# Second attention: the vector engine's squares one operation later, and the copy of the weighted sums moved from ScalarE to VectorE

## The chip, the cores and the metric

The kernel runs on one core of one Trainium2 chip. The metric is device time in microseconds (us) of one execution, the median of several. Lower is better. The engines are named as in the profile: PE (TensorE, matmuls; PEld is its weight loads), DVE (VectorE), ACT (ScalarE), POOL (GpSimd) and SP (SyncE, which only issues DMAs here).

## The reference, cut to what matters

The program is a stack of six layers over 4096 tokens of width 128: mixture of experts, causal attention, two mixtures of experts, a second attention, and a last mixture of experts. The change touches only the second attention. It is computed for each of 64 heads (4 batches of 16 heads, 1024 tokens each, 8 numbers to a head):

```python
S = jnp.einsum('bhnd,bhmd->bhnm', Q, K) / dh ** 0.5
W_tau = jax.nn.softmax(S, axis=-1)
W_sigma = 1.0 / ((1.0 + jnp.abs(S) / b_) ** 2 + t_ ** 2)
W_sigma = W_sigma / W_sigma.sum(axis=-1, keepdims=True)
tau = jnp.einsum('bhnm,bhmd->bhnd', W_tau, V)
sigma = jnp.einsum('bhnm,bhmd->bhnd', W_sigma, V)
f = 0.5 * tau + 0.5 * sigma
```

So every score is used twice: once through an exponential with the row's maximum taken off, and once as |S|, squared with an offset, then inverted.

## The kernel before, in words

`attend_both` (L1665 to L1979) holds five instruction streams written out by hand, one for each engine, which meet only through semaphores. Each engine works through its own stream in order: an instruction that waits holds up everything behind it on that engine.

The unit is a slot. A slot handles two blocks of 128 tokens (i = 0 and i = 1, its two halves) of a head, four slots to a head, 256 in all, plus a few at the end that only finish. One slot `j` works on different slots' data at once, each operation at its own lag (`LS, LT, LE, LP = 4, 6, 6, 7`):

- lag 0, the maxima: PE makes scores in PSUM tile `pm` (L1800); DVE reduces them to a row's maximum `mx` (L1958). Once in each half.
- lag 4, the absolute values: PE makes scores in `pa`; DVE clears their sign bit into the SBUF tile `sg` (L1967). Once in each half. Then, once in each slot, `sg` gets its square, sg times (sg + b): POOL does columns 0 to 831 of each half, in two instructions, first `shifted` = sg + b (L1758, "the shift" below) and then sg times `shifted` (L1761, "the product"); DVE does the columns 832 to 1023 of each half in one `scalar_tensor_tensor` (L1973, "the square" below).
- lag 6, the exponentials: PE makes scores in `pb`, ACT exponentiates them into `pt` (L1880), once in each half; ACT also turns the squares into weights with Ln (L1895, first half, which waits for both squares) and Exp (L1899, second half).
- lag 7 and 8, the weighing: PE multiplies V with `pt` and `sg` into one PSUM tile `po`, four matmuls in each half (L1817, `weigh`). In slot j's half i = 0 it does the second block of slot j-8, in half i = 1 the first block of slot j-7.

`pm`, `pa` and `pb` are single tiles. PE's order in each half is `pm`, `pb`, `pa`, `weigh`; a matmul group into `pm` waits for the reduction of the one before, one into `pa` for the absolute values before. DVE's order in a slot is maximum, absolute values, maximum, absolute values, square.

The slots of a head differ. Below they are called A (j mod 4 = 0), B, C and D (j mod 4 = 3):

- D: the weighing in its first half ends a head. ACT copies `po` to `osb` (L1887) after its first exponential. In the second half `weigh` starts the next head in the same `po`, so it waits for that copy (`o_sb`, L1815). After it PE turns `osb` with four transposes into `ptr` (L1863), which also waits for the copy.
- A: DVE normalises the turned sums between its first maximum and its first absolute values (`output`, L1934 to L1948, four small instructions, "the output"), and at the slot's end makes the negated maxima of another head (`negated`, L1914 to L1921, four small instructions, "the negation"). POOL makes two small copies for the next head (L1747, L1749) before its shift.

All these orders are written out by hand; no planner sets them.

Of the kernel before, what the change touches and what calls it, by code (L numbers as in the profile page):

```python
# [11 lines left out]
ALU = mybir.AluOpType  # L12
# [8 lines left out]
TT = T // P  # L21
# [1648 lines left out]
def attend_both(nc, tag, V, F, par, qd, kd, ident, stacks, cleared):  # L1670
# [11 lines left out]
    with ExitStack() as ctx:  # L1682
# [28 lines left out]
        def at(it, j, lag):  # L1711
            s = UNROLL * it + (j - lag)
            return None if isinstance(s, int) and not 0 <= s < SLOTS else s

        def head(it, j, lag):

            return RING * it + (j - lag) // PER
# [10 lines left out]
        def some(x, least=1):  # L1728

            return not (isinstance(x, int) and x < least)  # L1730

        with nc.Block() as block:

            @block.gpsimd
            def _(pool):
                nc.gpsimd.memset(Vh[:], 0.0).then_inc(vh_cleared, 1)
                pool.wait_ge(vh_cleared, 1)

                def body(it, j):
                    s = at(it, j, LS)  # L1740
                    if s is None:
                        return
                    h = head(it, j, LS)
                    if (j - LS) % PER == 0:
                        if some(h, 2):
                            pool.wait_ge(pv_done, TT * (h - 1))
                        nc.gpsimd.tensor_copy(parh[:, ((j - LS) // PER) % RING, :], par[:, h, :])\  # L1747
                            .then_inc(par_ready, 1)
                        nc.gpsimd.tensor_copy(Vh[:, ((j - LS) // PER) % 2, :, 0:DH + 1], V[:, h, :, :])\  # L1749
                            .then_inc(vh_ready, 1)  # L1750
                    buf = sg[(j - LS) % 4]
                    if some(s):
                        pool.wait_ge(sq_pool, s)
                    pool.wait_ge(par_ready, h + 1)
                    pool.wait_ge(abs_done, 2 * s + 2)
                    pool.nop(nofuse=True)
                    b2 = parh[:, ((j - LS) // PER) % RING, 0:1]
                    nc.gpsimd.tensor_scalar(shifted[:], buf[:, :, 0:CUT], b2, 1.0, ALU.add, ALU.mult)\  # L1758
                        .then_inc(shift_done, 1)
                    pool.wait_ge(shift_done, s + 1)  # L1760
                    nc.gpsimd.tensor_tensor(buf[:, :, 0:CUT], buf[:, :, 0:CUT], shifted[:], ALU.mult)\  # L1761
                        .then_inc(sq_pool, 1)

                slots(pool, body)
# [104 lines left out]
            @block.scalar  # L1869
            def _(act):  # L1870
                nc.scalar.preload_act_table_set("natural_log_exp_and_others")

                def body(it, j):
                    st, se, so = at(it, j, LT), at(it, j, LE), at(it, j, LP + 1)
                    for i in range(2):
                        if st is not None:
                            act.wait_ge(tau_mm, 2 * st + i + 1)
                            if some(st, 4):
                                act.wait_ge(pv_done, 2 * (st - 4) + i + 1)
                            nc.scalar.activation(pt[(j - LT) % 4][:, i, :], pb[:], ACT.Exp, scale=SC)\  # L1880
                                .then_inc(tau_exp, 1)
                        if i == 0 and so is not None and (j - LP - 1) % PER == PER - 1:
                            h = head(it, j, LP + 1)
                            act.wait_ge(pv_done, TT * h + TT)
                            if some(h):
                                act.wait_ge(o_turned, h)
                            nc.scalar.activation(osb[:], po[:], ACT.Copy).then_inc(o_sb, 1)  # L1887
                        if se is not None:
                            buf = sg[(j - LE) % 4]
                            if i == 0:  # L1890
                                h = head(it, j, LE)
                                act.wait_ge(sq_pool, se + 1)
                                act.wait_ge(sq_dve, se + 1)
                                act.wait_ge(par_ready, h + 1)
                                nc.scalar.activation(buf[:], buf[:], ACT.Ln,  # L1895
                                                     bias=parh[:, ((j - LE) // PER) % RING, 1:2]).then_inc(ln_done, 1)
                            else:
                                act.wait_ge(ln_done, se + 1)
                                nc.scalar.activation(buf[:], buf[:], ACT.Exp, scale=-1.0).then_inc(sig_done, 1)  # L1899

                slots(act, body)

            @block.vector
            def _(dve):
# [18 lines left out]
                def output(it, j, n):  # L1923

                    if (j - LP - 2) % PER != PER - 1 or at(it, j, LP + 2) is None:
                        return
                    h = head(it, j, LP + 2)
                    o = ptr[:].rearrange("p (c q k) -> p c q k", c=4, q=4)
                    scale = rz[:].unsqueeze(3).broadcast_to([P, 4, 4, DH])
                    if n == 0:  # L1930
                        dve.wait_ge(o_turned, h + 1)
                        if some(h):
                            dve.wait_ge(weighed, 2 * h)
                        nc.vector.reciprocal(rz[:], o[:, :, :, DH]).then_inc(rz_done, 1)  # L1934
                    if n == 1:
                        dve.wait_ge(rz_done, h + 1)
                        if some(h):
                            dve.wait_ge(f_done, h)
                        nc.vector.tensor_tensor(fw[:], o[:, :, 0:2, 0:DH], scale[:, :, 0:2], ALU.mult)\
                            .then_inc(weighed, 1)  # L1940
                        nc.vector.tensor_tensor(o[:, :, 2:4, 0:DH], o[:, :, 2:4, 0:DH], scale[:, :, 2:4], ALU.mult)\
                            .then_inc(weighed, 1)
                    if n == 2:
                        dve.wait_ge(weighed, 2 * h + 2)
                        nc.vector.tensor_tensor(F[:, :, h, :].rearrange("p (s c) d -> p s c d", s=2),
                                                o[:, :, 2:4, 0:DH].rearrange("p c s d -> p s c d"),
                                                fw[:].rearrange("p c s d -> p s c d"), ALU.add)\
                            .then_inc(f_done, 1)  # L1948

                def body(it, j):  # L1950
                    sm, ss = at(it, j, 0), at(it, j, LS)
                    for i in range(2):
                        if sm is not None:
                            t = 2 * (j % PER) + i
                            dve.wait_ge(max_mm, 2 * sm + i + 1)
                            if i == 0 and j % PER == 0 and some(sm, 2 * PER):
                                dve.wait_ge(rows_turned, head(it, j, 0) - 1)
                            nc.vector.tensor_reduce(mx[:, (j // PER) % 2, t:t + 1], pm[:], AX.X, ALU.max)\  # L1958
                                .then_inc(max_red, 1)
                        if i == 0:  # L1960
                            for n in range(3):
                                output(it, j, n)
                        if ss is not None:
                            dve.wait_ge(abs_mm, 2 * ss + i + 1)
                            if some(ss, 4):
                                dve.wait_ge(pv_done, 2 * (ss - 4) + i + 1)
                            nc.vector.tensor_scalar(sg[(j - LS) % 4][:, i, :].bitcast(I32), pa[:].bitcast(I32),  # L1967
                                                    SIGN_OFF, None, ALU.bitwise_and).then_inc(abs_done, 1)
                    if ss is not None:
                        h, buf = head(it, j, LS), sg[(j - LS) % 4]  # L1970
                        dve.wait_ge(abs_done, 2 * ss + 2)
                        dve.wait_ge(par_ready, h + 1)
                        nc.vector.scalar_tensor_tensor(buf[:, :, CUT:T], buf[:, :, CUT:T],  # L1973
                                                       parh[:, ((j - LS) // PER) % RING, 0:1], buf[:, :, CUT:T],
                                                       ALU.add, ALU.mult).then_inc(sq_dve, 1)
                    negated(it, j)

                slots(dve, body)
# [165 lines left out]
```

## Time and profile before

| | |
|---|---|
| median of 3 runs | 3061.43 us (3060.11 to 3062.47) |
| the profiled execution's own time | 3088.97 us |
| its span, first to last instruction | 3086.9 us |
| busy DVE, PE, ACT, POOL | 2546.7, 2456.0, 2250.8, 1999.4 us (83, 80, 73, 65% of the span) |
| the second attention, maxima first to last (L1958) | starts at 1241.3, last at 2770.2 us |

Busy is the time in which an engine executes; the rest is idle, mostly waiting. Shares over the whole span mix stages; the change must be read from the stretch of about 1240 to 2810 us, where the page shows DVE, ACT and POOL 9 tenths busy in each slice and PE 8 or 9. A timeline row gives start, duration, engine, line and operation, the tile written, the tile read, their shapes, and in brackets how long the engine was idle before it and who ended that.

### The profile page before, as it was taken

How to read it: one execution, taken by the hardware profiler on the slowest of the kernel's cores; microseconds unless marked ns; L12 is line 12 of the kernel's file. 1: busy time of each engine (PE TensorE's matmuls, PEld its weight loads, DVE VectorE, ACT ScalarE, POOL GpSimd, SP SyncE). 2: the span in 40 equal slices, each digit the busy share in tenths (PEclk: the TensorE clock that was granted, in tenths of full speed). 3: DMA queues.
4: the chain of work that ended last, by engine and by line, in shares of the span. 5: the costliest groups of instructions: out<-in, count | busy, mean ns of one | idle time of the engine just before them, and what ended most of it. 6: DMA issues, size and time to landing. Idle time of an engine off the chain costs nothing. (4 is left out here: it accounts for less than half of the span.)

```text
span 3086.9 us, 61248 instructions
## 1 busy us (share of the span) xinstructions
PE 2456.0 (80%) x18614; PEld 1025.5 (33%) x18614; DVE 2546.7 (83%) x4239; ACT 2250.8 (73%) x2441; POOL 1999.4 (65%) x1364
## 2 busy tenths in 40 slices
PE   2545999998476994688888888888888888885798
PEld 2542333334374662122222222222222222222466
DVE  4566888885467657799999999999999999996765
ACT  4332777776364553499999999999999999994454
POOL 4520222222453651599999999999999999995365
PEclk9976999999596997699999999999999999997799
DMA  3213101100111002000000000000000000000000
GB/s 110 58 51 102 30 27 29 28 28 10 41 55 28 1 0 83 19 13 14 14 12 12 12 14 13 12 12 12 15 12 12 12 13 14 12 4 0 1 11 17
DMA packets 77121, 74.42 MB, mean 24 GB/s; under 512 B 16096, under 2 KB 57576, under 8 KB 76880
## 3 DMA queue, kind: packets, MB, share of 16 engines
q1 hardware_dynamic: 72720, 64.20, 7.0%
q0 software_dynamic: 4288, 8.82, 0.9%
q8 instruction: 58, 0.95, 0.1%
q14 instruction: 55, 0.45, 0.1%
HBM read 47.77 MB, written 24.42 MB: 23 GB/s over the span
## 5 line engine op out<-in xcount | busy, mean ns | idle before, releaser
L1761 POOL TENSOR_TENSOR a_sg<-a_sg,a_shifted 128x1664 f32<-128x1664 f32 x256 | 955.4, 3732 | 21.4
L1958 DVE TENSOR_REDUCE a_mx<-a_pm 128x1 f32<-128x1024 f32 x512 | 619.5, 1210 | 22.0 <-PE a_pm L1800 21.9
L1967 DVE TENSOR_SCALAR a_sg<-a_pa 128x1024 int32<-128x1024 int32 x512 | 619.4, 1210 | 4.1 <-PE a_pa L1800 3.8
L1880 ACT ACTIVATE a_pt<-a_pb 128x1024 f32<-128x1024 f32 x512 | 523.5, 1023 | 108.6 <-PE a_pb L1800 108.4
L1817 PE MATMUL a_po<-a_pt,a_Vh 128*32 128x512 f32 x2048 | 540.6, 607 | 2.2 <-ACT a_sg L1899 2.2
L1817 PE MATMUL a_po<-a_sg,a_Vh 128*32 128x512 f32 x2048 | 540.6, 607 | 0.0
L1758 POOL TENSOR_SCALAR a_shifted<-a_sg,a_parh 128x1664 f32<-128x1664 f32 x256 | 470.4, 1837 | 102.3 <-DVE a_sg L1967 64.8
L1895 ACT ACTIVATE a_sg<-a_sg,a_parh 128x2048 f32<-128x2048 f32 x256 | 511.9, 1999 | 0.0
L1899 ACT ACTIVATE a_sg<-a_sg 128x2048 f32<-128x2048 f32 x256 | 489.9, 1914 | 0.0
L1800 PE MATMUL a_pm<-all_K,all_Q 96*128 96x512 bf16 x1024 | 315.9, 391 | 151.2 <-DVE a_mx L1958 124.1
L1579 ACT ACTIVATE a_pt<-a_ring 128x1024 f32<-128x1024 f32 (+2 forms) x384 | 313.6, 846 | 165.7 <-PE a_ring L1506 162.4
L1656 DVE TENSOR_REDUCE a_mx<-a_ring 128x2 f32<-128x1024 f32 (+3 forms) x384 | 359.3, 955 | 75.4 <-PE a_ring L1489 51.1
L1800 PE MATMUL a_pa<-all_Q,all_K 96*128 96x512 bf16 x1024 | 310.8, 385 | 83.5 <-DVE a_sg L1967 66.3
L1414 POOL TENSOR_SCALAR_AFFINE_SELECT a_pt<-a_pt 128x256 f32<-128x256 f32 x256 | 104.0, 406 | 370.7 <-ACT a_pt L1579 370.3
L1800 PE MATMUL a_pb<-all_Q,all_K 128*128 128x512 bf16 x1024 | 307.5, 381 | 6.0 <-ACT a_pt L1880 5.4
L1973 DVE SCALAR_TENSOR_TENSOR a_sg<-a_sg,a_parh 128x384 f32<-128x384 f32 x256 | 234.1, 915 | 15.7 <-POOL a_parh L1747 2.8
L1800 PEld LDWEIGHTS a_pm<-all_K,all_Q 96*128 96x128 bf16 x1024 | 63.5, 97 | 546.6 <-DVE a_mx L1958 523.3
L1523 PE MATMUL a_po<-a_pt,a_Vh 128*32 128x384 f32 (+3 forms) x1920 | 190.7, 435 | 1.9 <-POOL a_pt L1414 1.8
L900 ACT ACTIVATE f_sg<-f_psg 128x512 f32<-128x512 f32 x176 | 104.5, 594 | 116.7 <-PE f_psg L859 116.7
L1800 PEld LDWEIGHTS a_pa<-all_Q,all_K 96*128 96x128 bf16 x1024 | 79.3, 97 | 273.2 <-DVE a_sg L1967 232.7
L954 DVE TENSOR_TENSOR f_su<-f_psu,f_sg 128x512 f32<-128x512 f32 x144 | 98.7, 687 | 79.8 <-PE f_psu L859 74.5
L1506 PE MATMUL a_ring<-all_Q,all_K 51*128 51x512 bf16 (+2 forms) x768 | 131.8, 341 | 36.9 <-DVE a_mx L1656 32.1
(272 smaller groups left out, 4612.9 us busy)
## 6 DMA issues: line engine op xcount, KB each, us to landing
all_Q<-q_parts SPq DMA_DIRECT2D x256, 48.0 KB
all_K<-k_parts SPq DMA_DIRECT2D x256, 48.0 KB
k_parts<-p_parts SPq DMA_DIRECT2D x16, 384.0 KB, 2.6
all_Q<-a_rows SPq DMA_DIRECT2D x384, 2.0 KB
e_recs<-routed_rows SPq DMA_DIRECT2D x70, 64.5 KB, 1.8
n_xn<-expert_rows SPq DMA_DIRECT2D x16, 256.0 KB, 4.4
q_parts<-p_parts SPq DMA_DIRECT2D x16, 192.0 KB, 2.3
q_parts<-p_parts SPq DMA_DIRECT2D x8, 384.0 KB, 2.6
```

Source lines behind the costliest of these rows:

```text
L1579: nc.scalar.activation(pt[n % 4][:, :, ga:gb, c * P:CH], of_weight(y)[:, :, 0:(gb - ga) * width].rearrange("p u (g n) -> p u g n", n=width ...
L1656: nc.vector.tensor_reduce(mx[:, j % 2, half, :, strip_at(t)], of_maximum(y)[:, :, 0:min(CH, (t + 1) * P - half * CH)], AX.X, ALU.max).then ...
L1758: nc.gpsimd.tensor_scalar(shifted[:], buf[:, :, 0:CUT], b2, 1.0, ALU.add, ALU.mult)\
L1761: nc.gpsimd.tensor_tensor(buf[:, :, 0:CUT], buf[:, :, 0:CUT], shifted[:], ALU.mult)\
L1800: last = nc.tensor.matmul(out[:, lo:lo + CH], lhsT[0:rows_, t * P:(t + 1) * P], rhs[0:rows_, lo:lo + CH], start=True, stop=True)
L1817: last = nc.tensor.matmul(po[32 * q:32 * q + 32, :], Vh[:, ((j - lag) // PER) % 2, t, :], wts[:, i, half * CH:(half + 1) * CH], start=(t = ...
L1880: nc.scalar.activation(pt[(j - LT) % 4][:, i, :], pb[:], ACT.Exp, scale=SC)\
L1895: nc.scalar.activation(buf[:], buf[:], ACT.Ln, bias=parh[:, ((j - LE) // PER) % RING, 1:2]).then_inc(ln_done, 1)
L1899: nc.scalar.activation(buf[:], buf[:], ACT.Exp, scale=-1.0).then_inc(sig_done, 1)
L1958: nc.vector.tensor_reduce(mx[:, (j // PER) % 2, t:t + 1], pm[:], AX.X, ALU.max)\
L1967: nc.vector.tensor_scalar(sg[(j - LS) % 4][:, i, :].bitcast(I32), pa[:].bitcast(I32), SIGN_OFF, None, ALU.bitwise_and).then_inc(abs_done, 1)
L1973: nc.vector.scalar_tensor_tensor(buf[:, :, CUT:T], buf[:, :, CUT:T], parh[:, ((j - LS) // PER) % RING, 0:1], buf[:, :, CUT:T], ALU.add, AL ...
```

## The change

Three edits. The DVE square of a slot is issued one operation later: not at the end of the slot, but in the next slot behind its first maximum (and ahead of the output). POOL's product gets a second wait: besides its own shift it now waits for the DVE square of the same slot (`sq_dve`). The copy of `po` to `osb` leaves ACT; DVE does it in slot D between its second maximum and its second absolute values.

```diff
@@ pool
                     pool.wait_ge(shift_done, s + 1)
+                    pool.wait_ge(sq_dve, s + 1)
                     nc.gpsimd.tensor_tensor(buf[:, :, 0:CUT], buf[:, :, 0:CUT], shifted[:], ALU.mult)\
                         .then_inc(sq_pool, 1)
@@ act
-                        if i == 0 and so is not None and (j - LP - 1) % PER == PER - 1:
-                            h = head(it, j, LP + 1)
-                            act.wait_ge(pv_done, TT * h + TT)
-                            if some(h):
-                                act.wait_ge(o_turned, h)
-                            nc.scalar.activation(osb[:], po[:], ACT.Copy).then_inc(o_sb, 1)
@@ dve
+                def copy_out(it, j):
+
+                    if (j - LP - 1) % PER != PER - 1 or at(it, j, LP + 1) is None:
+                        return
+                    h = head(it, j, LP + 1)
+                    dve.wait_ge(pv_done, TT * h + TT)
+                    if some(h):
+                        dve.wait_ge(o_turned, h)
+                    nc.vector.tensor_copy(osb[:], po[:]).then_inc(o_sb, 1)
+
+                def square(it, j):
+
+                    s = at(it, j, LS + 1)
+                    if s is None:
+                        return
+                    h, buf = head(it, j, LS + 1), sg[(j - LS - 1) % 4]
+                    dve.wait_ge(abs_done, 2 * s + 2)
+                    dve.wait_ge(par_ready, h + 1)
+                    nc.vector.scalar_tensor_tensor(buf[:, :, CUT:T], buf[:, :, CUT:T],
+                                                   parh[:, ((j - LS - 1) // PER) % RING, 0:1], buf[:, :, CUT:T],
+                                                   ALU.add, ALU.mult).then_inc(sq_dve, 1)
@@ dve, body
                         if i == 0:
+                            square(it, j)
                             for n in range(3):
                                 output(it, j, n)
+                        else:
+                            copy_out(it, j)
@@ dve, after the two halves
-                    if ss is not None:
-                        h, buf = head(it, j, LS), sg[(j - LS) % 4]
-                        dve.wait_ge(abs_done, 2 * ss + 2)
-                        dve.wait_ge(par_ready, h + 1)
-                        nc.vector.scalar_tensor_tensor(buf[:, :, CUT:T], buf[:, :, CUT:T],
-                                                       parh[:, ((j - LS) // PER) % RING, 0:1], buf[:, :, CUT:T],
-                                                       ALU.add, ALU.mult).then_inc(sq_dve, 1)
                     negated(it, j)
```

## Rows read from the trace of the kernel before

**Rows 1.** Busy us of each engine in the steady stretch (window view).
```profile
core 0: us, PE busy (x) PEld busy (x) DVE busy (x) ACT busy (x) POOL busy (x), PEclk, DMA share, GB/s
1340.00:2700.00 1360.00, 1175.15 (x6624) 312.56 (x6625) 1332.29 (x1582) 1294.56 (x964) 1278.71 (x565) 1.00 0.04 13
```

**Rows 2.** Groups by line: busy us, mean ns of one, idle before and its releasers.
```profile
L1758 POOL TENSOR_SCALAR a_shifted<-a_sg,a_parh 128x1664 f32<-128x1664 f32 x256 | 470.4, 1837 | 102.3 <-DVE a_sg L1967 64.8 <-POOL a_sg L1761 32.2
...
L1973 DVE SCALAR_TENSOR_TENSOR a_sg<-a_sg,a_parh 128x384 f32<-128x384 f32 x256 | 234.1, 915 | 15.7 <-POOL a_parh L1747 2.8
...
L1887 ACT ACTIVATE a_osb<-a_po 128x512 f32<-128x512 f32 x64 | 38.2, 597 | 6.0 <-PE a_po L1817 3.6
```

**Rows 3.** Timeline of DVE from slot D's second maximum to the next D's.
```profile
2001.27 1.21 DVE L1958 TENSOR_REDUCE a_mx<-a_pm 128x1 f32<-128x1024 f32 x1
2002.40 1.21 DVE L1967 TENSOR_SCALAR a_sg<-a_pa 128x1024 int32<-128x1024 int32 x1
2003.65 1.20 DVE L1973 SCALAR_TENSOR_TENSOR a_sg<-a_sg,a_parh 128x384 f32<-128x384 f32 x1
2004.77 1.21 DVE L1958 TENSOR_REDUCE a_mx<-a_pm 128x1 f32<-128x1024 f32 x1
2005.90 0.24 DVE L1934 RECIPROCAL a_rz<-a_ptr 128x16 f32<-128x16 f32 x1
...
2006.93 1.22 DVE L1967 TENSOR_SCALAR a_sg<-a_pa 128x1024 int32<-128x1024 int32 x1
...
2009.20 1.21 DVE L1967 TENSOR_SCALAR a_sg<-a_pa 128x1024 int32<-128x1024 int32 x1
2010.45 0.62 DVE L1973 SCALAR_TENSOR_TENSOR a_sg<-a_sg,a_parh 128x384 f32<-128x384 f32 x1
...
2012.14 1.20 DVE L1958 TENSOR_REDUCE a_mx<-a_pm 128x1 f32<-128x1024 f32 x1
...
2016.77 0.62 DVE L1973 SCALAR_TENSOR_TENSOR a_sg<-a_sg,a_parh 128x384 f32<-128x384 f32 x1
2017.30 1.22 DVE L1958 TENSOR_REDUCE a_mx<-a_pm 128x1 f32<-128x1024 f32 x1
...
2025.33 1.21 DVE L1958 TENSOR_REDUCE a_mx<-a_pm 128x1 f32<-128x1024 f32 x1
```

**Rows 4.** Timeline of POOL beside them.
```profile
2000.69 3.74 POOL L1761 TENSOR_TENSOR a_sg<-a_sg,a_shifted 128x1664 f32<-128x1664 f32 x1
2004.68 1.68 POOL L1758 TENSOR_SCALAR a_shifted<-a_sg,a_parh 128x1664 f32<-128x1664 f32 x1 [0.25 <-POOL a_sg L1761]
2006.45 3.73 POOL L1761 TENSOR_TENSOR a_sg<-a_sg,a_shifted 128x1664 f32<-128x1664 f32 x1
...
2010.62 1.97 POOL L1758 TENSOR_SCALAR a_shifted<-a_sg,a_parh 128x1664 f32<-128x1664 f32 x1
...
2016.90 2.00 POOL L1758 TENSOR_SCALAR a_shifted<-a_sg,a_parh 128x1664 f32<-128x1664 f32 x1 [0.51 <-DVE a_sg L1967]
```

**Rows 5.** Timeline of PE, second half of slot D and on into A.
```profile
2001.41 0.60 PE L1800 MATMUL a_pa<-all_Q,all_K 96*128 96x512 bf16 x2
2001.94 0.62 PE L1817 MATMUL a_po<-a_pt,a_Vh 128*32 128x512 f32 x2
...
2002.94 0.66 PE L1863 MATMUL a_ptr<-all_ident,a_osb 128*128 128x128 f32 x4
2003.43 0.60 PE L1800 MATMUL a_pm<-all_K,all_Q 96*128 96x512 bf16 x2
...
2006.04 0.60 PE L1800 MATMUL a_pm<-all_K,all_Q 96*128 96x512 bf16 x2
```

**Rows 6.** Timeline of both engines where a maximum waited for its scores.
```profile
1296.13 0.60 PE L1800 MATMUL a_pm<-all_K,all_Q 96*128 96x512 bf16 x2
...
1296.77 1.22 DVE L1958 TENSOR_REDUCE a_mx<-a_pm 128x1 f32<-128x1024 f32 x1 [0.31 <-PE a_pm L1800]
```

**Rows 7.** Groups by line of DVE: instructions that read PSUM and write SBUF.
```profile
L963 DVE TENSOR_TENSOR f_hid<-f_psm,f_su 128x512 f32<-128x512 f32 x144 | 97.7, 680 | 1.7 <-POOL all_V L820 1.7
...
L1124 DVE COPY all_V<-p_psv 128x128 f32<-128x128 f32 x32 | 7.0, 281 | 0.0
```

More of the change, by code:

```diff
@@ L1873, in body @@
                 def body(it, j):
-                    st, se, so = at(it, j, LT), at(it, j, LE), at(it, j, LP + 1)
+                    st, se = at(it, j, LT), at(it, j, LE)
                     for i in range(2):
```

## The prediction, made before the changed kernel ran

> **What bounds the kernel now.** I first read the window view of the steady stretch: of 1360 us DVE is busy 1332, ACT 1295, POOL 1279, PE 1175 [rows 1]. DVE is 98% full, so whatever is added to it, or makes it wait, should show. Next, the groups by line: the square has a mean of 915 ns [rows 2], but the timeline shows only two durations, 0.62 us (A, B) and 1.20 us (C, D) [rows 3]. POOL's timeline says why: the 1.20 us square starts at 2003.65, while a product runs until 2000.69 + 3.74 = 2004.43, and it ends 0.42 us after that; the 0.62 us ones start before POOL's shift, and that shift then takes 1.97 or 2.00 us instead of 1.68 [rows 4]. So square and POOL exclude each other in both orders: whoever is second stands until the first is done. DVE loses 0.58 us in two slots of four.
>
> The head's period is 2025.33 - 2001.27 = 24.06 us [rows 3]. POOL is close behind: product start to next product 2006.45 - 2000.69 = 5.76 us where it never waits, and 0.19 us once a head for its two copies (product end 2010.18 to shift 2010.62, 0.44 instead of 0.25) [rows 4]: 4 x 5.76 + 0.19 = 23.23 us. The slack of POOL is 0.8 us a head.
>
> **The pieces, from the rows.** Issue to issue, DVE's maximum and absolute values take 1.13 us each (2001.27 to 2002.40), though each lasts 1.21; a free square 0.53 (2016.77 to 2017.30), a held one until 0.09 before its end; the output 2006.93 - 2005.90 = 1.03; the negation 2012.14 - 2010.45 - 0.53 = 1.16 [rows 3]. POOL: end of product to shift 0.25, end of shift to product 0.09, absolute values done to shift 2016.90 - 2016.77 + 0.03 = 0.16 [rows 3, 4]. PE: `pa` to `weigh` 0.53, `weigh` 1.00, transposes 0.49 (2002.94 to 2003.43); `pm` starts 0.06 after a maximum ends (2005.98 to 2006.04) [rows 3, 5], and a maximum that waits starts 0.64 after `pm` (1296.13 to 1296.77) [rows 6].
>
> **The change, part by part.** I write the new schedule of one head with the second maximum of slot D at 0.
>
> *The copy, slot D.* Off ACT: 0.60 us once a head [rows 2]. ACT idles 65 of 1360 us already [rows 1] and ends no wait of DVE or POOL, so this earns nothing. On DVE the nearest row of this size that reads PSUM and writes SBUF is 680 ns for 128x512; a 128x128 copy is 281 ns, and the two differ by 1.04 ns a column, a rate that a copy should share [rows 7]. Bounds: ACT's 0.60 and 0.75. I take 0.68, 0.60 issue to issue. It runs from 1.13 to 1.81. Its own wait is free: the last weighing lies ahead of `pm` in PE's order. But behind it hangs `weigh` of the second half, which must not overwrite `po`. Before, it started 2001.94 - 2001.27 = 0.67 after the maximum [rows 3, 5]; now at 1.81 + 0.06 = 1.87. Then transposes at 2.87, next `pm` at 3.36, and DVE's maximum of slot A at 4.00. DVE, which no longer has a square there, is free at 1.13 + 0.60 + 1.13 = 2.86: it stands for 1.14 us. The cover that hid PE's chain before was the square (the maximum came 3.50 after the last one).
>
> *Slot D's square and slot A.* Absolute values done at 1.73 + 1.21 = 2.94; shift 3.10 to 4.78; square issued at 4.00 + 1.13 = 5.13, POOL idle then, ends 5.75. The new wait holds the product until 5.85 (0.10 after the square; bounds 0.06 and 0.25), ends 9.58. DVE: output from 5.66, absolute values 6.69, maximum 7.82, absolute values 8.95, negation 10.08, maximum of B 11.24, square 12.37 to 12.99. The shift of A starts at the later of 9.58 + 0.44 and 10.16 + 0.21, 10.37, and ends 12.05, so this square too is free; product 13.09 to 16.82.
>
> *Slots B and C.* B's absolute values start at 12.90 and 15.16. The maximum of C comes not 1.13 behind: PE needs the first absolute values done (1.21), 0.05, `pa` 0.53, `weigh` 1.00, `pm` 0.64, in all 3.43 after 12.90, so 16.33, and its square is issued at 17.46. But POOL began B's shift at 16.82 + 0.25 = 17.07, until 18.75. The square stands behind it and ends at 18.75 + 0.42 = 19.17, 1.71 us long. Only then can the product start, 19.27 to 23.00. Before, nothing stood between shift and product. C repeats it 6.18 later: shift 23.25 to 24.93, square held until 25.35, product to 29.18. DVE goes on at 25.26, and the second maximum of D comes at 26.39. (POOL's next shift is then due at 29.43, DVE's work at 29.49: the schedule closes.)
>
> *Sum.* 26.39 - 24.06 = 2.33 us a head. The maxima of 64 heads fill 1529 us, 63.5 periods; the first and last slots lack weighing or maxima, so I count 62: 62 x 2.33 = 144 us. The profiled execution is 3088.97 us, with 2.07 around its span of 3086.9; it would become 3233. It lies 27.5 above the median of 3061.43. The added time is in engines' instructions and waits, so it is put on the median: 3205 us.
>
> **The Trainium skill.** That a square stands behind a *shift* is my extension: in the rows the square waits for a product (two SBUF inputs), and the shift (one tensor) waits for a square [rows 4]. The Trainium skill, "SBUF — State Buffer", section "Who interferes with whom", says that a DVE instruction with two SBUF inputs contends with a GpSimd one that reads SBUF, and that the second to issue blocks fully. By that rule the shift holds the square, which is the 3205 above; if a one-input instruction held nothing, the sum would be the 3072 of rival 1. The trace agrees in the order it has.
>
> **Bounds.** A shift that does not hold a square gives the lower end (rival 1). The wait's release, twice on the chain (A's and B's product), 0.06 or 0.25 instead of 0.10: -0.1 to +0.3 a head. The copy 0.60 or 0.75: -0.08 to +0.07. PE's restart after a wait 0.06, or up to 0.4: up to +0.3. So 2.15 to 3.0 a head, 3195 to 3247.
>
> **Rivals.**
> 1. *Squares are not behind shifts.* Either a shift doesn't hold them, or POOL is a little later than worked out (the margin in B and C is 17.46 - 17.07 = 0.39 us) and the square goes first. Unheld: after 17.46 follow 17.99, 21.42, 22.55, 23.08, and the period is 24.21: +0.15, 62 x 0.15 = 9 us, 3071 to 3072. Square first, and then, as now, held 0.58 behind a product in two slots: +1.31, 81 us, 3143. For it: the small margin. Against it: both engines hang on the same square's end, so the margin doesn't drift. Chance 0.13.
> 2. *Faster: the copy is hidden and the squares are free.* If PE lost nothing by `weigh` waiting, DVE would need 24.21 - 1.14 = 23.07, POOL 23.23 binds, -0.83 a head: -51 us, 3010. It decides if DVE's idle before A's maximum is near zero. Against it: PE goes from `weigh` through transposes to `pm` without a gap today [rows 5]. Chance 0.05.
> 3. *POOL becomes the sole bound and is woken late.* If its product starts 0.5 after a square instead of 0.10, the two waits on the chain add 0.8 a head: 3.13 x 62 = 194, 3255. Against it: 0.16 for the shift today. Chance 0.12.
>
> Forecast 0.70, its own range 3190 to 3230. The range 3120 to 3245 takes in the upper part of rival 1 and the lower part of rival 3. A measurement can tell about 0.2%, 6 us: faster 0.05 (rival 2), same 0.03 (the low edge of rival 1), slower 0.92.
>
> **What would show it.** In the after trace: the square 0.62 us in two slots of a head (for D and A) and about 1.7 us in the two others, mean near 1.16; the shift 1.68 everywhere; POOL idle before its product, released by the square, 1.0 us twice and 0.5 us twice a head; DVE idle 1.1 us before A's maximum on `pm`, and PE's weights for `po` waiting for DVE's `osb` 1.2 us; the copy at 0.68 us; period 26.4 us. It is wrong if squares behind a shift last 0.62 us, if slot A's maximum isn't late, or if the period is under 25.

## The result and the profile after

The changed kernel takes 3261.56 us (median of 4 runs, 3260.98 to 3266.71) against 3061.36 for the kernel before: ratio 1.066, 95% interval 1.0647 to 1.0672. It is 200.2 us slower; 143.6 were forecast (3205, range to 3245). The direction held, and so did the steps of the hand schedule wherever the granted clock was 1.00; one term was missing, about 56 us, and the range ended 17 us short of the result.

All of it lies in the second attention. Its maxima now run from 1212.2 to 2942.3 us, 1730.1 us; before, 1241.3 to 2770.2, 1528.9. That is 201.2 us more. (In the profiled execution of the kernel before, the stages ahead of it took 29 us more than in that of after, and its own time lay 27.5 us above its median; so putting the difference on the median was right.)

The window view of after, columns as in [rows 1]:

```profile
core 0: us, PE busy (x) PEld busy (x) DVE busy (x) ACT busy (x) POOL busy (x), PEclk, DMA share, GB/s
1340.00:2640.00 1300.00, 1043.46 (x5481) 281.51 (x5573) 1190.03 (x1380) 1074.50 (x763) 1039.90 (x478) 0.94 0.04 11
```

No engine is full any more: DVE fell from 98 to 92%, POOL from 94 to 80%. Everything became less busy while the time grew, so the engines wait for each other more than before. And the granted clock is 0.94 where it was 1.00, which was not forecast.

The groups by line (columns as in [rows 2]) name the waits:

```profile
L1762 POOL TENSOR_TENSOR a_sg<-a_sg,a_shifted 128x1664 f32<-128x1664 f32 x256 | 954.6, 3729 | 269.4 <-DVE a_sg L1963 268.9
...
L1818 PE MATMUL a_po<-a_pt,a_Vh 128*32 128x512 f32 x2048 | 573.6, 640 | 77.5 <-DVE a_osb L1953 75.2 <-ACT a_sg L1894 2.2
...
L1758 POOL TENSOR_SCALAR a_shifted<-a_sg,a_parh 128x1664 f32<-128x1664 f32 x256 | 424.3, 1657 | 102.1 <-DVE a_sg L1987 69.4 <-POOL a_sg L1762 32.6
L1975 DVE TENSOR_REDUCE a_mx<-a_pm 128x1 f32<-128x1024 f32 x512 | 621.3, 1214 | 145.8 <-PE a_pm L1801 145.8
...
L1963 DVE SCALAR_TENSOR_TENSOR a_sg<-a_sg,a_parh 128x384 f32<-128x384 f32 x256 | 297.1, 1161 | 0.5 <-POOL a_parh L1747 0.3
...
L1953 DVE COPY a_osb<-a_po 128x512 f32<-128x512 f32 x64 | 43.1, 674 | 12.7 <-PE a_po L1818 12.7
```

The shift is no longer held (mean 1657 ns, it was 1837 [rows 2]); the square's mean is 1161 ns (1.16 forecast, 915 before); POOL stands 269 us for it; PE stands 75 us for the copy; the copy is 674 ns (0.68 forecast). DVE stands 146 us for `pm` ahead of its maxima.

Here is DVE of after from slot B's square to slot A, the rows that answer to [rows 3]:

```profile
2005.11 1.69 DVE L1963 SCALAR_TENSOR_TENSOR a_sg<-a_sg,a_parh 128x384 f32<-128x384 f32 x1
...
2011.31 1.68 DVE L1963 SCALAR_TENSOR_TENSOR a_sg<-a_sg,a_parh 128x384 f32<-128x384 f32 x1
...
2014.05 1.21 DVE L1975 TENSOR_REDUCE a_mx<-a_pm 128x1 f32<-128x1024 f32 x1
2015.18 0.67 DVE L1953 COPY a_osb<-a_po 128x512 f32<-128x512 f32 x1
2015.78 1.21 DVE L1987 TENSOR_SCALAR a_sg<-a_pa 128x1024 int32<-128x1024 int32 x1
2018.12 1.23 DVE L1975 TENSOR_REDUCE a_mx<-a_pm 128x1 f32<-128x1024 f32 x1 [1.14 <-PE a_pm L1801]
2019.26 0.61 DVE L1963 SCALAR_TENSOR_TENSOR a_sg<-a_sg,a_parh 128x384 f32<-128x384 f32 x1
...
2040.42 1.21 DVE L1975 TENSOR_REDUCE a_mx<-a_pm 128x1 f32<-128x1024 f32 x1
...
2046.24 1.22 DVE L1975 TENSOR_REDUCE a_mx<-a_pm 128x1 f32<-128x1024 f32 x1 [2.89 <-PE a_pm L1801]
```

And POOL beside it, to be read with [rows 4]:

```profile
2004.75 1.65 POOL L1758 TENSOR_SCALAR a_shifted<-a_sg,a_parh 128x1664 f32<-128x1664 f32 x1 [0.26 <-POOL a_sg L1762]
2006.95 3.72 POOL L1762 TENSOR_TENSOR a_sg<-a_sg,a_shifted 128x1664 f32<-128x1664 f32 x1 [0.55 <-DVE a_sg L1963]
2010.93 1.66 POOL L1758 TENSOR_SCALAR a_shifted<-a_sg,a_parh 128x1664 f32<-128x1664 f32 x1 [0.25 <-POOL a_sg L1762]
2013.14 3.72 POOL L1762 TENSOR_TENSOR a_sg<-a_sg,a_shifted 128x1664 f32<-128x1664 f32 x1 [0.56 <-DVE a_sg L1963]
...
2020.02 3.73 POOL L1762 TENSOR_TENSOR a_sg<-a_sg,a_shifted 128x1664 f32<-128x1664 f32 x1 [1.21 <-DVE a_sg L1963]
...
2027.13 3.73 POOL L1762 TENSOR_TENSOR a_sg<-a_sg,a_shifted 128x1664 f32<-128x1664 f32 x1 [1.11 <-DVE a_sg L1963]
```

The square at 2005.11 is issued 0.36 us into the shift of 2004.75 to 2006.40, and ends 0.40 after it. The product of 2006.95 could have started at 2006.49 (0.09 after the shift). DVE's copy of 2015.18 runs inside the product of 2013.14 to 2016.86 and still takes 0.67 us: the product does not hold it. From D's second maximum (2014.05) to A's first (2018.12) are 4.07 us (4.00 forecast); to D's second maximum of the next head (2040.42) are 26.37 us (26.39 forecast).

The next slot D is another matter: its A comes at 2046.24, 5.82 us after 2040.42, and DVE stands 2.89 us. PE of after in that slot:

```profile
2042.37 1.07 PE L1818 MATMUL a_po<-a_pt,a_Vh 128*32 128x512 f32 x2 [1.21 <-DVE a_osb L1953]
...
2043.20 1.10 PE L1818 MATMUL a_po<-a_pt,a_Vh 128*32 128x512 f32 x2
...
2044.24 1.12 PE L1864 MATMUL a_ptr<-all_ident,a_osb 128*128 128x128 f32 x4
2045.15 1.06 PE L1801 MATMUL a_pm<-all_K,all_Q 96*128 96x512 bf16 x2
```

The window view gives the granted clock of the two slots, the late one first:

```profile
2042.00:2048.00 6.00, 5.63 (x22) 1.99 (x26) 3.11 (x5) 1.51 (x2) 2.88 (x2) 0.50 0.00 0
2015.50:2020.00 4.50, 4.00 (x27) 1.43 (x28) 3.36 (x5) 2.17 (x3) 3.01 (x2) 1.00 0.00 0
```

In the late slot TensorE is at 1.2 GHz, in the other at 2.4. The chain on which DVE stands is weighing, transposes and `pm`. From the first weighing to `pm` it takes 2.78 us (2042.37 to 2045.15) instead of 1.49 (1.00 + 0.49 [rows 5]), and from `pm` to DVE's maximum 1.09 (2045.15 to 2046.24) instead of 0.64: 1.74 us more in all. 31 of the 63 head periods are like this. The trace has 31 stretches at 0.5 while these heads run, 200.6 us together; each begins 1.0 to 1.9 us after the second maximum of a slot D, one in each late head and none in the others.

The clock falls at 2041.6. In the 5.2 us ahead of that PE did much the same as at the same place of the head before, where the clock stayed up (columns as in [rows 1]):

```profile
2010.00:2015.20 5.20, 3.52 (x18) 0.84 (x17) 5.20 (x6) 4.63 (x5) 4.39 (x3) 1.00 0.00 0
2036.40:2041.60 5.20, 3.49 (x18) 0.82 (x17) 5.20 (x6) 4.63 (x5) 4.39 (x3) 1.00 0.00 0
```

### The profile page after: what moved, and what is told of

It is laid out like the page before. It is cut to its first block and busy times, and to the rows that moved or that the text cites. A ratio compares the mean times of both kernels' runs of the same rounds, so it can differ in the third digit from the quotient of the medians.

```text
span 3259.3 us, 61437 instructions
## 1 busy us (share of the span) xinstructions
PE 2519.3 (77%) x18487; PEld 1047.2 (32%) x18614; DVE 2643.7 (81%) x4303; ACT 2227.9 (68%) x2377; POOL 1952.2 (60%) x1364
## 5 line engine op out<-in xcount | busy, mean ns | idle before, releaser
L1818 PE MATMUL a_po<-a_pt,a_Vh 128*32 128x512 f32 x2048 | 573.6, 640 | 77.5 <-DVE a_osb L1953 75.2
L1818 PE MATMUL a_po<-a_sg,a_Vh 128*32 128x512 f32 x2048 | 573.5, 640 | 0.0
L1801 PE MATMUL a_pa<-all_Q,all_K 96*128 96x512 bf16 x1024 | 323.5, 399 | 232.2 <-DVE a_sg L1987 231.9
L1758 POOL TENSOR_SCALAR a_shifted<-a_sg,a_parh 128x1664 f32<-128x1664 f32 x256 | 424.3, 1657 | 102.1 <-DVE a_sg L1987 69.4
L1801 PE MATMUL a_pm<-all_K,all_Q 96*128 96x512 bf16 x1024 | 329.5, 405 | 53.6 <-DVE a_mx L1975 38.2
L1801 PE MATMUL a_pb<-all_Q,all_K 128*128 128x512 bf16 x897 | 291.9, 396 | 14.9 <-ACT a_pt L1881 7.6
L1963 DVE SCALAR_TENSOR_TENSOR a_sg<-a_sg,a_parh 128x384 f32<-128x384 f32 x256 | 297.1, 1161 | 0.5 <-POOL a_parh L1747 0.3
L1818 PEld LDWEIGHTS a_po<-a_pt,a_Vh 128*32 128x32 f32 x2048 | 78.5, 111 | 303.7 <-issue 240.2
```

Source lines behind the costliest of these rows:

```text
L1801: last = nc.tensor.matmul(out[:, lo:lo + CH], lhsT[0:rows_, t * P:(t + 1) * P], rhs[0:rows_, lo:lo + CH], start=True, stop=True)
L1818: last = nc.tensor.matmul(po[32 * q:32 * q + 32, :], Vh[:, ((j - lag) // PER) % 2, t, :], wts[:, i, half * CH:(half + 1) * CH], start=(t = ...
```

## Experiments

Each comparison is with the kernel before on the same chip. "The head's period" is read from D's second maximum to the next D's. What an experiment does not name is as in the kernel that it starts from. Except in e3, e7 and e8, every fourth head is 0.1 to 0.2 us longer than the period given.

**e1, the copy alone.** The kernel before, with `copy_out` of the change on DVE and ACT's copy gone; square and product as before.

> The kernel before with one edit: DVE copies the weighted sums out in slot D. The changed kernel's trace shows the head's period alternating between 26.4 or 26.6 us, as forecast, and 28.1 us, where the granted clock is at 0.5 from the copy's wait on. Theory (clock): TensorE's clock falls because PE does less in a head's period than before, held in slot D behind the copy and in B and C behind the held squares. Here only the copy's hold is left: A's maximum starts 4.00 us after D's second one instead of 3.50, so 24.03 + 0.5 = 24.55 us a head, 62 x 0.5 = 31 us, 3092 us, and the clock stays at 1.0 if slot D's hold alone is not enough to bring it down. Rival (the hold in slot D alone brings the clock down, whatever the other slots do): every second head gets 1.75 us more, 31 x 1.75 = 54, 3147 us. Rival (the copy costs nothing): 3061 us.

Measured: 3131.8 us, ratio 1.023 (1.0213 to 1.0247), +71.8. Where the clock stays up the head's period is 24.64 us (24.03 before); A's maximum comes 4.08 after D's (4.00 forecast). D's square, which now comes later, is no longer held (0.62 instead of 1.20 us), so the copy's 0.60 us on DVE costs next to nothing by itself, and the 0.6 us a head are DVE's wait for PE's chain. But 23 of 63 heads have 5.45 to 5.82 us from D's maximum to A's, 35.6 us more in all. So with the copy's hold alone the clock falls too, though not in every second head: between theory and rival. DVE's waits in two neighbouring heads of e1:

```profile
2015.44 1.22 DVE L1962 TENSOR_REDUCE a_mx<-a_pm 128x1 f32<-128x1024 f32 x1 [0.59 <-PE a_pm L1800]
...
2041.67 1.23 DVE L1962 TENSOR_REDUCE a_mx<-a_pm 128x1 f32<-128x1024 f32 x1 [2.08 <-PE a_pm L1800]
```

The first stands 0.59 us at full clock, the second 2.08 with the clock at 0.5 for a part of PE's chain.

**e2, the squares alone.** The change without its copy: `copy_out` out, ACT's copy back.

> The kernel before with the other two edits: DVE's square one operation later and POOL's product waits for it; the copy stays on ACT. The same hand schedule without the copy: D's square is issued at 3.93 after D's second maximum while the shift runs (3.04 to 4.69), is held to 5.11 instead of ending at 5.75, and all that follows is 0.64 us earlier: period 26.39 - 0.64 = 25.75 us, 62 x 1.72 = 107 us, 3168 us at full clock. Theory (clock): PE has no hold of 1.2 us in slot D, so the clock stays at 1.0 and 3168 us stands. Rival (the low activity of the whole period brings the clock down): 1.75 us more in each second head, 3222 us. Rival (the gain was lost to the copy alone, squares are harmless): 3061 us.

Measured: 3166.6 us, ratio 1.035 (1.0334 to 1.0368), +106.6, against 107 forecast. That this is so close is partly luck: the head's period is 25.70 us, not 25.75, and the theory on the clock was wrong. Its mean over the stretch is 0.98, not 1.00: there are 15 short stretches at 0.5, 51 us together. But each begins 7.6 to 8.6 us after D's second maximum, in slot A, behind the chain that DVE waits for; A's maximum comes at 2.79 to 2.90 in every head of the steady stretch. Nine heads are longer, by at most 0.6 us, about 4 us in all. So a low clock costs much only where PE's chain ends last; and it can fall without any hold by the copy. The groups of e2:

```profile
L1762 POOL TENSOR_TENSOR a_sg<-a_sg,a_shifted 128x1664 f32<-128x1664 f32 x256 | 955.4, 3732 | 178.0 <-DVE a_sg L1959 177.6
...
L1959 DVE SCALAR_TENSOR_TENSOR a_sg<-a_sg,a_parh 128x384 f32<-128x384 f32 x256 | 330.0, 1289 | 0.7 <-POOL a_parh L1747 0.6
```

The mean square is even longer than in the changed kernel (1289 against 1161): slot D's square, without the copy ahead of it, is issued in a shift too (1.20 us). POOL's waits for the square, 178 us, are 0.55 us in three slots of a head and 1.11 in the fourth.

**e3, the product without its new wait.** e2 with one line less:

```diff
                     pool.wait_ge(shift_done, s + 1)
-                    pool.wait_ge(sq_dve, s + 1)
```

> As e2_square_only, but POOL's product does not wait for DVE's square (they touch different columns). Theory (whoever waits takes the port at the next change of instruction, as the square did behind a product): the square goes first when the shift ends, the product stands 0.4 us behind it and shows as about 4.1 us; 0.1 us less idle in B, C and D: about 3150 us. Rival (the product, 0.09 us behind the shift, keeps the port): a square issued in a shift is held through the product too, 5.5 us long in B and C, the head's period grows by over 6 us: above 3450 us.

Measured: 3531.0 us, ratio 1.154 (1.1518 to 1.1557). The time is the rival's, the mechanism is neither's. DVE of e3, then POOL:

```profile
2003.06 0.74 DVE L1958 SCALAR_TENSOR_TENSOR a_sg<-a_sg,a_parh 128x384 f32<-128x384 f32 x1
...
2016.72 3.84 DVE L1958 SCALAR_TENSOR_TENSOR a_sg<-a_sg,a_parh 128x384 f32<-128x384 f32 x1
```

```profile
2001.75 1.65 POOL L1758 TENSOR_SCALAR a_shifted<-a_sg,a_parh 128x1664 f32<-128x1664 f32 x1 [3.99 <-DVE a_sg L1980]
2003.48 3.91 POOL L1761 TENSOR_TENSOR a_sg<-a_sg,a_shifted 128x1664 f32<-128x1664 f32 x1
...
2016.44 3.70 POOL L1761 TENSOR_TENSOR a_sg<-a_sg,a_shifted 128x1664 f32<-128x1664 f32 x1
```

The square of 2003.06 was issued in the shift, ended 0.40 after the shift's end at 2003.40, and the product issued at 2003.48 took 3.91 instead of 3.72: at a change of POOL's instruction the waiting square goes first, as my theory had it. But with POOL not waiting, about half of the squares (125 of 256 last over 3 us) come when the product has already begun, and are held through it: 3.84 us for the one of 2016.72. So the new wait is not a careless addition: once the square is issued late, it keeps the product from starting ahead of it, at the cost of POOL's waits given under e2. The granted clock of e3 was 0.89 over 1340 to 2640 us; how much of its time is the clock's is not separated here.

**e4, the changed kernel with PE kept busy.** In slot D, second half, ahead of the scores into `pa`. `fill` (a new helper, not shown) issues the same two matmuls, twice:

```diff
+                            if i == 1 and (j - LP - 1) % PER == PER - 1 and at(it, j, LP + 1) is not None:
+                                fill(pa, K[rs], Q[rs], 2 * ((j - LS) % PER) + i, 96)
                             scores(pa, K[rs], Q[rs], 2 * ((j - LS) % PER) + i, 96, abs_mm)
```

> The changed kernel with PE kept busy in slot D's second half: the two score matmuls into pa are issued three times with the same result, only the last signals DVE, four more matmuls of about 0.22 us at a point where PE then waits 1.2 us for the copy. Theory (clock): the matmuls take the place of waiting, the granted clock stays higher, and the missing 56 us come back: all heads at 26.4 to 26.6, 3207 us; if they only delay the fall, some heads stay at 28.1. Rival (the alternation of the heads' periods comes from a buffer or a DMA that turns every second head, and the clock falls as its result): 3262 us or, with PE's extra work on the path, above.

Measured: 3221.7 us, ratio 1.053 (1.051 to 1.0545): about 40 us faster than the changed kernel, by more work. 8 heads are still late, 12.6 us in all; without them it would be 3209 (3207 forecast). The window view of e4:

```profile
1340.00:2640.00 1300.00, 1058.68 (x5920) 293.37 (x5917) 1221.39 (x1417) 1103.14 (x783) 1067.14 (x491) 0.99 0.04 11
```

**e5, the same filler in e1.**

> e1_copy_only with the filler of e4_after_filled (in slot D's second half the two score matmuls into pa are issued three times with the same result). e1 has 24.64 us a head where the granted clock stays at 1.0, and about 1.5 us more in 24 of 63 heads whose slot D meets a clock of 0.5. Theory (clock): PE's wait for the copy brings the clock down; with the filler in its place nearly all heads take 24.64: 62 x 0.61 = 38 us over before, about 3099 us. Rival (the filler is on PE's path, or the clock falls for another reason): 3132 us or more.

Measured: 3097.2 us, ratio 1.012 (1.0104 to 1.0138), 34.6 us faster than e1. All heads of the steady stretch are at 24.64 to 24.77, and the clock, low as in every kernel when the second attention begins (until 1247 us), does not fall again in it. (The expectation speaks of 24 late heads of e1; they are 23, the 24th stretch at 0.5 lies in another slot.) The copy's cost without the clock is 36 us, with it 72. PE's mean busy share, from the window view of 1340 to 2640 us, does not order these runs: it is 85% in e1, where 23 heads are late, and 81% in e4, where 8 are.

```profile
1340.00:2640.00 1300.00, 1139.85 (x6382) 313.40 (x6374) 1247.41 (x1528) 1180.13 (x844) 1194.26 (x527) 1.00 0.04 12
```

**e6, the square ahead of the shift.** e2 with the wait moved:

```diff
                     pool.wait_ge(abs_done, 2 * s + 2)
+                    pool.wait_ge(sq_dve, s + 1)
                     pool.nop(nofuse=True)
...
                     pool.wait_ge(shift_done, s + 1)
-                    pool.wait_ge(sq_dve, s + 1)
```

> e2_square_only with the wait for DVE's square moved from POOL's product to POOL's shift. Theory (the loss of e2 is that a square issued in a shift is held to its end and POOL waits for it, 0.55 us of POOL's time in B and C and more in A and D): now the square goes ahead of the shift; it can only be held behind the product of the slot before, which it meets later in its run. Hand schedule: B and C take 5.57 + 0.42 = 6.0 us instead of 6.18, A and D are no longer held behind a shift, period about 25.2 us, 62 x 1.2 = 75 us, 3136 us. Rival (what costs is that POOL waits for DVE at all, wherever): POOL's shift and product then both stand behind a late square, the same or more than e2, 3167 us or above.

Measured: 3146.9 us, ratio 1.028 (1.0264 to 1.0298), 20 us better than e2, period 25.30 us (25.2 forecast). The square (mean 1215 ns) is now held behind the product of the slot before, B's and C's and D's; A's is free:

```profile
2005.69 1.55 DVE L1959 SCALAR_TENSOR_TENSOR a_sg<-a_sg,a_parh 128x384 f32<-128x384 f32 x1
...
2003.08 3.74 POOL L1762 TENSOR_TENSOR a_sg<-a_sg,a_shifted 128x1664 f32<-128x1664 f32 x1
```

The product ends at 2006.82, the square at 2007.24, 0.42 after it. With the wait in either of the two places, a square one operation late meets a POOL instruction in three slots of four; the order decides which.

**e7 and e8, less on POOL.** The kernel before with `CUT = 25 * T // 32` and `CUT = 24 * T // 32` instead of 26.

> The kernel before with CUT = 25 * T // 32: POOL squares 800 columns of each half instead of 832, DVE 224 instead of 192. Theory (in C and D the square stands 0.58 us behind a product that is late by POOL's own length): shift and product get 4% shorter, each square 0.07 us longer. Holds fall from 0.58 to about 0.38 in C and 0.31 in D: -0.2 -0.27 + 4 x 0.07 = -0.2 us a head, 12 us, 3048 us. Rival (DVE is the bound, so each column moved to it costs): +0.27 us a head, 3077 us.

> As e7_cut25 with CUT = 24 * T // 32. Theory: holds of about 0.15 in C and 0.04 in D: -0.43 -0.54 + 4 x 0.135 = -0.43 us a head, 27 us, 3034 us. Rival (DVE is the bound): +0.54 us a head, 3094 us.

Measured: e7 3053.9 us, ratio 0.9973 (0.9963 to 0.9984); e8 3045.1 us, ratio 0.9948 (0.9931 to 0.9965). Both are under 1% faster than the kernel before, by more than their intervals. The sign is the theory's; the sizes are 7 of 12 us and 16 of 27 us. The groups of e8:

```profile
L1761 POOL TENSOR_TENSOR a_sg<-a_sg,a_shifted 128x1536 f32<-128x1536 f32 x256 | 885.9, 3460 | 21.4
...
L1973 DVE SCALAR_TENSOR_TENSOR a_sg<-a_sg,a_parh 128x512 f32<-128x512 f32 x256 | 221.1, 863 | 14.3 <-POOL a_parh L1747 1.3
```

A third more columns, and the mean square is shorter than before (863 against 915 ns [rows 2]): holds went down faster than work went up. In C and D it still lasts 0.95 and 0.97 us where a free one lasts 0.75, so 0.2 is left of each hold where I had 0.15 and 0.04. (e7: C's and D's squares 1.07, a free one 0.69, so 0.38 is left of each where I had 0.38 and 0.31.)

## Why the prediction was right and wrong, point by point

- *Square and POOL exclude each other, the shift too.* Right. B's and C's squares last 1.69 and 1.68 us (1.71 forecast), D's and A's 0.60 to 0.61 (0.62). "A square behind a shift" had no row before. The Trainium skill, "SBUF — State Buffer", section "Who interferes with whom", says that a DVE instruction with two SBUF inputs contends with a GpSimd one that reads SBUF. The trace of after agrees: the square ends 0.40 us after the shift does. Rival 1 (squares not behind shifts) is out.
- *The product waits.* Right: 0.55 us idle in B and C, 1.21 and 1.11 in D and A (1.0 forecast).
- *The copy.* Right: 0.67 us, PE's weighing held for 1.21, A's maximum late by 1.14 at full clock, as worked out (0.68, 1.2 and 1.14).
- *The sum 2.33 us a head.* Right at full clock: 26.37 us, against 24.03 before (the 24.06 of the forecast was one of the longer heads), so 2.34. Every fourth head has 26.60; those 14 add 3 us.
- *Two edits, separately.* The squares alone cost 106.6 us (e2), the copy alone without the clock 35.8 (e5): 142.4 us, and 144 was the sum for both. (e2 holds about 4 us of low clock.)
- *Wrong: "PE's restart after a wait 0.06, or up to 0.4: up to +0.3", and no line on the clock at all.* The step that failed is the term of PE's chain in slot D: I took `weigh` 1.00, transposes 0.49 and 0.64 for `pm` from rows at a granted clock of 1.00 [rows 1, 5, 6] and did not ask whether PE, busy 1175 of 1360 us before and made to stand by both edits, keeps it. It did not. At 0.5 the three take 2.78 and 1.09, in all 3.87 us instead of 2.13, where the bound allowed 0.3. Over the 31 late heads the excess over 4.08 us is 53.5 us; 144 + 53.5 + 3 = 200.5, measured 200.2, closer than terms rounded to 0.01 us a head deserve. That it is the clock and not a buffer that turns every second head is shown by the stretches at 0.5, one in each late head and in no other, and by e4 and e5: adding matmuls where PE stood removed most or all of the late heads, and the low clock with them.
- *Rival 3 (POOL woken late)* gave 3255, near the result, by a cause that did not occur: POOL's product follows the square by 0.15 us. Rival 2 (faster) is out: PE's chain had no slack.

What stays open: why the clock falls in every second head in the changed kernel and in 23 of 63 in e1. PE's work of the few us before is the same in a head where it falls and in one where it does not (3.49 and 3.52 of 5.20 us busy). The runs show only that in these two kernels it falls around the copy's hold and stays up, or falls less often, when matmuls fill it; in e2, without that hold, it falls at another place.

## What to carry to other kernels

Where two engines exclude each other, look at which instruction of the other is running at the moment of issue; moving the short one later by one operation put it from a collision that costs 0.58 us into one that costs 1.07 and made the other engine wait too. A copy that frees an accumulator belongs on the engine that can do it at once: on DVE, which was 98% busy, it held the next matmuls by 1.2 us a head, and DVE's next maximum behind them. When a change makes TensorE stand, price its chain at the lower clock as well, and use it as an end of the range.

## What the runs showed of the hardware that was not expected

- A low clock costs by place, not by length: 51 us at 0.5 in e2, behind the chain that DVE waits for, cost about 4 us; 200.6 us in the changed kernel, on that chain, cost 53.
- More matmuls made a kernel faster: four of them a head where PE waited, about 40 us (e4) and 35 us (e5), by keeping the clock up.
- A waiting DVE instruction goes first when POOL changes instruction, even if POOL's next is ready 0.08 us later (e3): POOL's is then stretched by 0.2 us (3.91 instead of 3.72).
- The order of issue decides the price of an exclusion: the same square costs 0.58 us behind a product that is nearly done, 1.07 in a shift, and up to 3.2 when the product has just begun (e3), and it holds POOL's shift by 0.3 when it goes first.
